# Softmax pass: turned rows in four PSUM banks in place of two, decays in SBUF

## What is computed

```python
def _L0_gnn_ref(feat, src, dst, W, b):
    m = relu(feat[src]) + EPS                    # a row of 96 features for each edge
    seg_max = segment_max(m, dst)
    ex = exp(m - seg_max[dst])
    denom = segment_sum(ex, dst)
    msg = segment_sum(ex / denom[dst] * m, dst)  # softmax over the edges of a node
    return (feat + msg) @ W + b

x = layernorm(x + _L0_gnn_ref(x, src, dst, W, b))
x = layernorm(x + L1(x))       # edge features, a matrix on each message, sums by destination
x = layernorm(x + L2(x))       # two mean aggregations
x = layernorm(x + L3(x))       # two mean aggregations
```

## Time and profile before

| | us |
|---|---|
| timed runs, median of 3 | 4446.39 |
| timed runs, lowest and highest | 4443.10, 4448.91 |
| profiled execution, span | 5171.8 |
| busy in the span: PE, DVE, ACT, POOL | 3159.9, 2679.3, 1560.3, 2510.8 |
| softmax pass, first to last start of L1695 | 114.4 to 1261.9 |

### The profile page before, as it was taken

One profiled execution on the slowest core, in us unless ns is written; L12 is line 12 of the kernel. 1 busy time (PEld: TensorE's weight loads), 2 busy tenths in 40 slices (PEclk: granted clock), 3 DMA queues, 4 the chain that ended last, 5 costly groups with the idle time before them and its releaser, 6 DMA issues.

```text
span 5171.8 us, 61853 instructions
## 1 busy us (share of the span) xinstructions
PE 3159.9 (61%) x18737; PEld 2317.1 (45%) x18737; DVE 2679.3 (52%) x5868; ACT 1560.3 (30%) x3684; POOL 2510.8 (49%) x2587
## 2 busy tenths in 40 slices
PE   1555555554755555555555554111159999999999
PEld 0333333333534344344344333100047777788777
DVE  4888888888645555555555556300001254433333
ACT  1777777776222222222222222100000011111000
POOL 7666666664666666666666666777720000000000
PEclk9999999999986667667667666555579999999999
DMA  5555555555134444444444443100037666666776
GB/s 183 192 198 191 195 194 194 192 192 164 56 98 111 112 121 111 116 117 111 114 118 112 111 118 85 58 0 0 13 126 282 215 218 245 247 248 251 259 276 228
DMA packets 387596, 797.88 MB, mean 154 GB/s; under 512 B 207412, under 2 KB 264600, under 8 KB 361128
## 3 DMA queue, kind: packets, MB, share of 16 engines
q1 hardware_dynamic: 239330, 586.35, 33.9%
q0 software_dynamic: 82320, 90.28, 7.9%
q10 hardware_dynamic: 65718, 118.62, 6.2%
HBM read 581.03 MB, written 213.92 MB: 154 GB/s over the span
## 4 chain that ended last, share of the span: by engine, by line
PE 25%; issue 23%; SPq 19%; DVE 3%; another core or an unknown queue 1%; DMA 0%; ACTq 0%; ACT 0%; DVEq 0%; POOL 0%
PE ps L1181 18%; SPq L626 14%; PE ps L1111 6%; SPq L601 1%; SPq L596 1%; SPq L622 1%; SPq L607 1%; SPq L617 1%; PE ps L1064 1%; ACTq L64 0%; DMA area<-adj 0%; PE ps L1083 0%; PE ps L1056 0%; DVE second L1650 0%
## 5 line engine op out<-in xcount | busy, mean ns | idle before, releaser
L770 POOL DMA_INDIRECT area<-src_table,early x784 | 752.5, 960 | 469.6 <-remote 225.5
L770 POOL DMA_INDIRECT area<-relu_table,early x784 | 739.6, 943 | 421.3 <-issue 212.4
L953 PE MATMUL ps<-ident,area 96*128 96x96 f32 x2352 | 441.4, 356 | 804.3 <-issue 555.4
L953 PEld LDWEIGHTS ps<-ident,area 96*128 96x128 f32 x2352 | 355.2, 213 | 939.2 <-issue 782.4
L1181 PE MATMUL ps<-second,area 128*128 128x288 bf16 x5194 | 652.1, 286 | 0.2 <-DVE second L1823 0.2
L1682 DVE TENSOR_TENSOR_SCAN area<-flags,area,ps 96x512 f32<-96x512 int8 x196 | 250.0, 1276 | 647.6 <-issue 552.0
L1181 PEld LDWEIGHTS ps<-second,area 128*128 128x128 f16 x5194 | 509.0, 98 | 128.5 <-DVE second L1823 0.5
L1650 DVE SCALAR_TENSOR_TENSOR second<-second,area,ps 128x512 bf16<-128x512 f32 x784 | 538.1, 741 | 0.0
L857 POOL DMA_INDIRECT adj<-out_ring x390 | 395.5, 1014 | 127.8 <-issue 127.8
L781 POOL DMA_INDIRECT adj<-copies_ring,cell_ring x392 | 388.6, 991 | 125.6 <-issue 118.9
L1111 PE MATMUL ps<-early,area 128*128 128x288 bf16 x2401 | 322.0, 292 | 204.9 <-issue 204.9
(11 more groups left out here) (330 smaller groups left out, 4709.0 us busy)
## 6 DMA issues: line engine op xcount, KB each, us to landing
area<-adj SPq DMA_DIRECT2D x147, 1632.0 KB
area<-adj SPq DMA_DIRECT2D x55, 1568.0 KB
adj<-early SPq DMA_DIRECT2D x102, 816.0 KB
soft_sums<-out_ring ACTq DMA_DIRECT2D x196, 384.0 KB
second<-key_dram SPq DMA_DIRECT2D x98, 512.0 KB
area<-dst_table SPq DMA_DIRECT2D x784, 48.0 KB
sums<-out_ring ACTq DMA_DIRECT2D x196, 192.0 KB
second<-caps_dram SPq DMA_DIRECT2D x98, 192.0 KB
```

Source lines behind the costliest of these rows:

```text
L770: pool.indirect_dma_start(out=src_rows[:, s, c, :], out_offset=None, in_=gather_table[p], in_offset=bass.IndirectOffsetOnAxis(ap=src_cols[ ...
L953: last = nc.tensor.transpose(ps[:, b, c * F:(c + 1) * F], r[:, (s * CH + c) * P:(s * CH + c + 1) * P], ident[0:F, 0:F])
```

## The change

The turned rows of a tile lie in bank `TURNED_BANKS[s]`, one of 0, 1, 4 and 5, so that four tiles have banks of their own; `turn` waits for the weighing of tile t-4, the last user of its bank. The banks 4 and 5 become free because `rose`, the decays, goes to a new pair of SBUF buffers, `decay`, cut out of `second`. Bank 4 holds a sum of the index computation that VectorE reads before the pass; so TensorE waits for `index_made` ahead of tile 2. On no engine does the order of instructions change: rows stand as they stood, with `ps` replaced by `second` in two ScalarE instructions and two VectorE scans of each tile.

```diff
--- before.py
+++ after.py
@@ -217,6 +217,7 @@
         caps = soft(F, RING * TE // 2).bitcast(bf16).rearrange("p (s e) -> p s e", s=RING)
         weight = soft(F, 2 * TE).rearrange("p (b e) -> p b e", b=2)
         weighted = soft(F, 2 * TE).rearrange("p (b e) -> p b e", b=2)
+        decay = soft(F, 2 * TE).rearrange("p (b e) -> p b e", b=2)
         message = parts_of(second)
         h_ring = message(F, 2 * TE).rearrange("p (b e) -> p b e", b=2)
         rank_hot = message(P, 2 * TE).rearrange("p (b e) -> p b e", b=2)
@@ -327,7 +328,7 @@
         def projected_pack(b):
             return ps[:, 4 + 2 * b:6 + 2 * b, :].rearrange("p b (k n) -> p (b k) n", n=2 * P)
 
-        DECAY_BANK = 4
+        TURNED_BANKS = (0, 1, 4, 5)
         ROW_NUMBERS, WEIGHTS_BANK = 4, 5
         weigh_words = bank(WEIGHTS_BANK, P, (TE + (CH - 1) * P) // 2)
         weigh_ps = weigh_words.bitcast(bf16)
@@ -920,9 +921,11 @@
                     t = u * RING + s
                     wait(pe, src_gathered[s], (p * EI + u + 1) * 16 * CH)
 
-                    wait(pe, e["weighed"] if kind == SOFT else e["summed"], t - 1)
+                    wait(pe, e["weighed"], t - RING + 1)
+                    if t == 2:
+                        pe.wait_ge(index_made, 1)
                     for c in range(CH):
-                        last = nc.tensor.transpose(ps[0:F, s % 2, c * P:(c + 1) * P], src_rows[:, s, c, :], ident[:, :])
+                        last = nc.tensor.transpose(ps[0:F, TURNED_BANKS[s], c * P:(c + 1) * P], src_rows[:, s, c, :], ident[:, :])
                     last.then_inc(e["turned"], 1)
 
                 def score(u, s):
@@ -1262,7 +1265,7 @@
                     relu_and_stats(relu_dump, bank(6 + s % 2, F), col["b_edge"][:, :], ef_sum, ef_sq, t, valid_edges(u, s),
                                    e["hrelu"], e["squared"])
                     wait(act, e["scored"], t + 1)
-                    rise, rose, sank = weight[:, s % 2, :], bank(DECAY_BANK + s % 2, F), weight[:, s % 2, :]
+                    rise, rose, sank = weight[:, s % 2, :], decay[:, s % 2, :], weight[:, s % 2, :]
                     nc.scalar.activation(rose, rise, ACT.Relu).then_inc(e["parted"], 1)
                     act.wait_ge(e["parted"], 2 * t + 1)
                     nc.scalar.activation(sank, rise, ACT.Relu, scale=-1.0).then_inc(e["parted"], 1)
@@ -1692,23 +1695,23 @@
                         v.tensor_copy(last_max[:, 0:1], last_max[:, RING * TE:RING * TE + 1]).then_inc(e["wrapped"], 1)
                         dve.wait_ge(e["wrapped"], u)
 
-                    v.tensor_tensor_scan(out=last_max[:, 1 + s * TE:1 + (s + 1) * TE], data0=bank(b, F), data1=caps[:, s, :],
+                    v.tensor_tensor_scan(out=last_max[:, 1 + s * TE:1 + (s + 1) * TE], data0=bank(TURNED_BANKS[s], F), data1=caps[:, s, :],
                                          initial=last_max[:, s * TE:s * TE + 1], op0=ALU.max, op1=ALU.min)\
                      .then_inc(e["maxed"], 1)
                     dve.wait_ge(e["maxed"], t + 1)
-                    v.tensor_tensor(weight[:, b, :], bank(b, F), last_max[:, s * TE:(s + 1) * TE], ALU.subtract)\
+                    v.tensor_tensor(weight[:, b, :], bank(TURNED_BANKS[s], F), last_max[:, s * TE:(s + 1) * TE], ALU.subtract)\
                      .then_inc(e["scored"], 1)
 
                 def soft_scan(u, s):
                     t, b = u * RING + s, s % 2
                     dve.wait_ge(e["expd"], t + 1)
-                    v.tensor_tensor(weighted[:, b, :], weight[:, b, :], bank(b, F), ALU.mult).then_inc(e["weighed"], 1)
+                    v.tensor_tensor(weighted[:, b, :], weight[:, b, :], bank(TURNED_BANKS[s], F), ALU.mult).then_inc(e["weighed"], 1)
                     wait(dve, e["back"], t - RING + 1)
                     wait(dve, e["summed"], t)
-                    v.tensor_tensor_scan(out=slot(sum_ring, s), data0=bank(DECAY_BANK + b, F), data1=weight[:, b, :],
+                    v.tensor_tensor_scan(out=slot(sum_ring, s), data0=decay[:, b, :], data1=weight[:, b, :],
                                          initial=last_of(sum_ring, s), op0=ALU.mult, op1=ALU.add)
                     dve.wait_ge(e["weighed"], t + 1)
-                    v.tensor_tensor_scan(out=slot(num_ring, s), data0=bank(DECAY_BANK + b, F), data1=weighted[:, b, :],
+                    v.tensor_tensor_scan(out=slot(num_ring, s), data0=decay[:, b, :], data1=weighted[:, b, :],
                                          initial=last_of(num_ring, s), op0=ALU.mult, op1=ALU.add).then_inc(e["summed"], 1)
 
                 if kind == MESSAGE:
```

## The result

The changed kernel takes 4503.07 us (median of 4 runs, 4501.91 to 4504.84) against 4444.75 (4 runs): a ratio of 1.0128, 95% interval 1.0116 to 1.0141. It is 58 us slower, and 37 us above the upper end of the range.

What follows compares the result with a forecast made beforehand. The softmax pass was taken as bound by ScalarE or POOL; ScalarE's 196 x 0.046 = +9.0 us, or 0 if POOL binds, other terms 0, gave +6: 4446.4 + 6 = 4452 us, range 4395 to 4466.

Steps and rivals of the forecast that it cites:

- What bounds the pass: Softmax pass, tile without waits: VectorE needs 4.87 us, ScalarE 4.94, POOL 4.99; the sum took ScalarE as the bound.
- "remote" waits: VectorE's L1695 waits about 2 us with releaser "remote", 153.7 us in 81 tiles; taken as part of the recording.
- The earlier turning: TensorE's `turn` waits for the weighing of t-4 in place of t-2, moving L925 up at most 2.86 us; worth 0.
- `index_made`: TensorE's new wait at tile 2, ahead of the whole pass: it ends earlier than the old one; cost 0.
- ScalarE's side: L1266 and L1269 with decays in SBUF: +0.024 to +0.079 us a tile, taken +0.046, so 4.94 becomes 4.99.
- VectorE's side: Scans L1708 and L1711 reading SBUF alone: 0 to 0.11 us less each, no loss, worth 0 behind ScalarE.
- What would make it wrong: A median lower by 40 us or more, or higher by over 20 us, meaning scans suffer from two SBUF streams.
- The one on the slower side: ScalarE's L1266 to L1271 pay for both moves: 0.079 us a tile, 15.5 us more, 4462; chance 0.26.
- The late news: TensorE's counts reach VectorE's L1695 late in timed runs too: gain 42 to 153.7 us, 4293 to 4404; chance 0.22.
- VectorE's scans give nothing back: Rival with VectorE as bound in timed runs: L1708 and L1711 give back 20 us, at most 43; 4427; chance 0.10.
- the change does what it says: Rival denying this: TensorE's turning comes hardly earlier, only ScalarE's small cost is left, 4446 to 4455; chance 0.06.

Runs made afterwards that it cites:

- second recording: The unchanged kernel before, recorded once more beside the changed kernel: its recording spans 4440.5 us, as its timed runs do.
- first recording: The unchanged kernel before, as recorded for the prediction: a span of 5171.8 us, against a timed median of 4446.39 us.

## Why the prediction was wrong, point by point

- *What bounds the pass.* Right: POOL's 4.99 us of the earlier trace rows is the tile of the second recording (4.992), and "remote" waits were rightly kept out of the sum. But the sum then went by ScalarE ("POOL's rhythm may be among the things that the recorder slows"); it wasn't, POOL was the bound.
- *The earlier turning* and *`index_made`*, both 0: right. The run with three banks and the decays left in PSUM gives 0.9999; the pass starts at 96.1 us against 96.4.
- *ScalarE's side*: the durations were right, L1266 583 to 625 ns (forecast 610 to 632) and L1269 577 to 615 (near 610). The term was right in size too: ScalarE's tile grows by 44 ns (forecast 46), nearly all of it at L1266, and the 9 us that this would cost as the bound are 6.2 us where POOL is out of the way, and 0 (1.0002) where POOL is the bound. The Trainium skill's 42 ns for each of the two ("Perfetto Trace Analysis", Optimizing Scalar/DVE Operations) are engine-busy times; from start to start the traces agree for L1266 (37 ns more) and not for L1269 (2 ns more).
- *VectorE's side*: **this is the step that failed.** "A loss I exclude because that row, two SBUF streams in and one out, shows none per element. Either way VectorE falls below ScalarE and POOL ... worth 0." For the scans' own durations this was nearly right: 1278 and 1261 ns in place of 1273 and 1254, neither shorter, as the 1162 of the one-partition row had it, nor longer to speak of. But the price of the edit wasn't on VectorE. It was charged to POOL, whose 4.99 us stood in the sum as unchanged, and POOL had no room. The first recording has the interaction, at the very instruction of the earlier trace rows, which reads one SBUF tensor as both its inputs:

```profile
40.19 1.78 DVE L1503 TENSOR_TENSOR_SCAN early<-area 1x784 f32<-1x784 f32 x1
40.72 2.01 POOL L756 DMA_INDIRECT out_ring<-node_rows_dram,early  x1 [0.30 <-issue]
```

  A gather of another line, which takes 944 ns in the median, starts 0.53 us into the scan, takes 2.01 us and ends 0.76 us after the scan's end (40.19 + 1.78 + 0.76 = 42.73 = 40.72 + 2.01), just as the held ones of after. The row was read for the scan's own duration alone, and the gathers' price was put at 0 in place of a bound.
- Such a bound could have been made from that row. If a gather that starts during a scan waits for its end, then with 4 gathers a tile, one each 1.25 us, a scan of 1.27 us holds about one gather, for half its length on average: about 2 x 0.6 us a tile, an estimate of 196 x 1.2 = 235 us if the two fall at random, against the 57 that came. The range would have had an upper end that far away, and a slower case larger than ScalarE's 15 us.
- *What would make it wrong*: the text named a median more than 20 us higher as the sign "that the scans suffer from reading two streams of SBUF". The sign came; the scans don't suffer, the gathers beside them do.
- *The rivals.* The one on the slower side had the wrong place: ScalarE's L1266 to L1271 get as much longer as it said, but behind POOL. The late news is not in the timed runs; VectorE's scans give nothing back; and the change does what it says, since TensorE's turning no longer waits for VectorE. So none of the rivals came.

The Trainium skill has a rule that should have raised the question, "SBUF — State Buffer", Who interferes with whom: a VectorE instruction with both inputs in SBUF takes its second one through a read interface that it shares with GpSimd, and contends with a GpSimd instruction that reads SBUF. By the same page's section SBUF: two separate sides, whoever is first has the shared pair for the whole instruction. The section doesn't say that the issue of an indirect DMA is such an instruction. The traces agree on one side: a gather that comes second ends 757 ns after the scan's end, to within 10 ns in 117 of 117 cases. They differ on the other: a first scan that starts while a gather runs isn't longer (1274 to 1276 ns), and one in whose first 90 ns a gather starts is longer by no more than about 70 ns (1345 against 1274), not by the 944 ns of the gather. That the shared interface is the cause here is not shown; the runs show the hold alone.

## What to carry to other kernels

Before an operand is moved from PSUM to SBUF to free a bank, look at what the reading VectorE instruction then reads: if both its inputs lie in SBUF and GpSimd issues indirect DMAs beside it, price the gathers and not only the instruction, and look in the trace for the longest of them, not at their mean: the held gather beside L1503 stood in the trace before the change. An engine whose instructions follow each other with nothing but "issue" between them has no room, even if another looks as busy, and any edit that can touch its durations needs a price there. If two SBUF inputs can't be avoided, shorter VectorE instructions hold the gathers for less: with two halves the loss fell from 58 to 24 us here, in one run, and the 24 are what the halves cost VectorE.

## What was not expected of the hardware

- An indirect DMA's issue on POOL (945 ns alone) that starts more than 90 ns into a two-SBUF-input scan ends 757 ns after the scan does, up to 1951 ns in all; one that started before the scan, within the scan's first 60 ns or in its last 190 ns is not longer, and between 60 and 90 ns both occur. What it needs at that point, its list in `early` or room to write, no run here tells apart.
- Not scans alone do it. In the first recording an elementwise instruction with two SBUF inputs, L1478, holds a gather that starts 0.06 us into it until 0.82 us after its end (28.11 + 3.42 + 0.82 = 32.35 = 28.17 + 4.18):

```profile
28.11 3.42 DVE L1478 TENSOR_TENSOR second<-second,area 128x3136 f32<-128x3136 f32 x1 [0.36 <-ACT area L1194]
28.17 4.18 POOL L756 DMA_INDIRECT out_ring<-node_rows_dram,early  x1 [0.30 <-issue]
```

- A scan of 96 x 512 takes 1273 ns with one input in PSUM and 1278 with both in SBUF: no access cost is saved.
- Half the scans made 84% of the loss (49 of 58 us): what the stops cost is not in proportion to the number of instructions that can stop a gather. That it goes by where the two engines' rhythms meet is argued, not shown.
